# The state-space block's norm worked in pieces inside the first feed-forward, with its input weights fused there and its residual bias added chunk by chunk

## The reference

```
x = x + attention(layernorm(x))
x = x + experts_0(layernorm(x))      # 8 experts, top 2, and a shared expert of two halves
x = x + state_space(layernorm(x))
x = x + experts_1(layernorm(x))
layernorm(x) = (x - mean) / sqrt(var + 1e-5)
state_space(x):  h = x @ fc1_w.T + fc1_b;  xz = h @ in_proj_w.T;  xc, z = split(xz)
                 u = silu(conv over 4 tokens of xc + conv_b)
                 dt, B, C = u @ x_proj_w.T, dt = softplus(dt @ dt_proj_w.T + dt_proj_b)
                 scan over tokens;  y = (y + u * D) * silu(z)
                 return y @ out_proj_w.T @ fc2_w.T + fc2_b
```

## Time and profile before

| | |
|---|---|
| median of 3 runs | 1396.83 us |
| profiled execution, its own time | 1397.44 us |
| its span, first to last instruction | 1395.6 us |
| mean granted clock of PE | 0.937 |
| busy in the span: PE, DVE, ACT, POOL | 88%, 78%, 61%, 41% |
| feed-forward, from about 500 to 749 us of the span | PE 99% busy from 700 to 740 us |
| norm block, 749 to 765 us | PE 8.9, DVE 10.4, ACT 6.1, POOL 8.0 us busy of 16 |

### The profile page before, as it was taken

One profiled execution on the slowest core, in us unless ns is written; L12 is line 12 of the kernel. 1 busy time (PEld: TensorE's weight loads), 2 busy tenths in 40 slices (PEclk: granted clock), 3 DMA queues, 4 the chain that ended last, 5 costly groups with the idle time before them and its releaser, 6 DMA issues. The chain is left out here.

```text
span 1395.6 us, 23364 instructions
## 1 busy us (share of the span) xinstructions
PE 1230.7 (88%) x8438; PEld 643.8 (46%) x8438; DVE 1090.8 (78%) x1318; ACT 851.2 (61%) x1506; POOL 574.8 (41%) x428
## 2 busy tenths in 40 slices
PE   4936999999899989989996866999999999976998
PEld 2411333334333434444543334555555556564665
DVE  5768999989799555867455766999999999864554
ACT  2523899989799742222222678989999899512221
POOL 2320010000100236656665114888888888820000
PEclk9965999999999999999997897999999999985999
DMA  4331111311211165323361001223232223101231
GB/s 111 113 115 31 55 60 48 104 56 55 75 54 50 41 93 143 114 91 113 103 116 23 0 5 49 93 94 100 91 103 94 91 94 103 61 29 24 60 62 38
DMA packets 70525, 103.16 MB, mean 74 GB/s; under 512 B 12598, under 2 KB 42246, under 8 KB 70422
## 3 DMA queue, kind: packets, MB, share of 16 engines
q1 hardware_dynamic: 69126, 100.47, 25.1%
q10 hardware_dynamic: 1296, 1.33, 0.4%
HBM read 88.00 MB, written 13.37 MB: 73 GB/s over the span
## 5 line engine op out<-in xcount | busy, mean ns | idle before, releaser
L638 DVE TENSOR_REDUCE att_found<-PS 128x2 f32<-128x1024 f32 (+2 forms) x288 | 333.2, 1218 | 20.9 <-PE PS L747 19.0
L714 ACT ACTIVATE att_prob<-PS 128x512 f32<-128x512 f32 x576 | 313.6, 596 | 46.1 <-PE PS L769 34.4
L1930 POOL TENSOR_TENSOR ms_ch<-xnT,ms_c_rows 128x1024 f32<-128x1024 f32 x103 | 243.7, 2367 | 45.4 <-PE PS L1840 33.3
L1840 PE MATMUL PS<-ms_ch,ident_sb 128*128 128x512 f32 x512 | 241.2, 593 | 1.0 <-POOL ms_ch L1930 1.0
L1891 DVE TENSOR_TENSOR_SCAN xnT<-xnT,PS 128x1024 f32<-128x1024 f32 x103 | 231.0, 2267 | 7.2 <-PE PS L1831 7.1
L1869 ACT ACTIVATE ms_scaled<-m_dtu_turns,m_bt 128x256 f32<-128x256 f32 x448 | 191.6, 495 | 29.3 <-PE PS L1831 29.3
L788 PE MATMUL PS<-att_prob,att_v 128*32 128x256 f32 (+1 forms) x2560 | 185.0, 376 | 2.8 <-ACT fr_out L703 2.6
L1831 PEld LDWEIGHTS PS<-ident_sb,ms_scaled 128*128 128x128 f32 x1024 | 119.3, 142 | 81.4 <-DVE xnT L1891 37.9
L747 PE MATMUL PS<-kr,qr 55*128 55x128 bf16 (+4 forms) x1152 | 121.7, 293 | 31.0 <-PEq L260 15.8
L1831 PE MATMUL PS<-ident_sb,ms_scaled 128*128 128x128 f32 x1024 | 135.4, 276 | 11.1 <-ACT ms_scaled L1869 5.6
L1262 ACT ACTIVATE f_h<-PS,e_w_b 128x512 f32<-128x512 f32 x64 | 44.0, 687 | 140.1 <-PE PS L1413 136.9
(11 more groups left out here) (225 smaller groups left out, 1724.9 us busy)
## 6 DMA issues: line engine op xcount, KB each, us to landing
ms_c_rows<-bc_rows_dram SPq DMA_DIRECT2D x64, 512.0 KB, 3.7
f_gate_row<-gate_rows_dram SPq DMA_DIRECT2D x64, 256.0 KB, 3.5
f_mask_row<-mask_rows_dram SPq DMA_DIRECT2D x64, 128.0 KB, 3.1
...
```

The lines of the kernel that those rows point to most:

```text
L638: dve.tensor_reduce(found[:, :, pair, first:first + (n - 1) * step + 1:step], PS[:, bank:bank + 2, :].rearrange("p r (w n) -> p r w n", w= ...
L714: act.activation(prob[:, step % PROB_RING * GH + h, :], PS[:, SCORE_BANK + unit % SCORE_RING, :], ACT.Exp, scale=float(D) ** -0.5).then_in ...
L1840: last = pe.matmul(PS[:, Y_BANK + 2 * half + q, :], g.ident[:, :], ch[:, half, q * CH:(q + 1) * CH], start=n == 0, stop=n == NS - 1)
L1930: pool.tensor_tensor(ch[:, half, :], decay_then_h(s, half), c_rows[:, s % C_RING, :], ALU.mult).then_inc(ch_ready, 1)
```

## The change

Four things are done.

1. The norm of the state-space block is taken out of its own block. For sequences 0, 1 and 2 it is done by `Front` in the feed-forward, as batches 4, 5 and 6, in chunks 5, 6 and 7: moments at experts 1 and 2, root on POOL behind the sum of expert 3, two tiles on DVE at each of experts 5, 6, 7 and the next chunk's 0, transposes at that chunk's experts 0 and 2, stores at 2 and 4. Batch 7 (sequence 3) follows behind the last chunk, and so do the last two tiles, the transposes and the stores of batch 6.
2. The weights fc1, in_proj, fc1_b, conv_w and conv_b are loaded by SP at the start of the feed-forward into a new SBUF row (`shared_row`), and the fused weights are computed at chunk 4: PE at expert 0, ACT's copies at expert 2.
3. The other weights of the state-space block are loaded by SP at the start of `mamba_in`, and its engines wait for them behind the convolution.
4. POOL adds fc2_b to X in eight pieces, one behind each `m_dt`.

```diff
     def turn_bank(self, b, k):
-        return (k, 2 + k, k, 1 - k)[b]
+        return (k, 2 + k, k, 1 - k)[b] if b < B else k
...
+    def normalize_half(self, dve, b, k, part):
+        dve.wait_ge(self.rstd_ready, b + 1)
+        dve.wait_ge(self.transposed, CPB * (b - 1) + k + 1)
+        self.normalize_tiles(dve, b, k, range(part * TPC // 2, (part + 1) * TPC // 2))
...
+        if b >= B:
+            pe.wait_ge(self.x_stored, CPB * (b - 1) + k + 1)
...
+        NORM_AT = 5
+
+        def norm_slot(b):
+
+            return NE * (NORM_AT + b - B)
...
         def _(sp):
+            for dst, src in early.pairs:
+                sp.dma_start(dst, src).then_inc(early.loaded, 16)
             for c in range(NCH):
...
+                    if c >= NORM_AT and e == 3:
+                        f.root(pool, B + c - NORM_AT)
+            f.root(pool, 2 * B - 1)
...
+                    if (c, e) == (4, 2):
+                        act.wait_ge(fused, 1)
+                        act.activation(early.in_proj.rearrange("p a b -> p (a b)"), PS[:, FUSED, :], ACT.Copy).then_inc(fused_stored, 1)
+                        act.activation(early.b_in_x, PS[:, FUSED_B, 0:2 * DI], ACT.Copy).then_inc(fused_stored, 1)
+                    for b in range(B, 2 * B - 2):
+                        for part in range(CPB):
+                            if 0 <= e < NE and NE * c + e == norm_slot(b) + 10 + 2 * part:
+                                f.store_x(act, b, part)
             chunks(act, chunk)
+            for b in range(2 * B - 2, 2 * B):
+                for part in range(CPB):
+                    f.store_x(act, b, part)
...
+                for b in range(B, 2 * B - 1):
+                    slot = NE * c + e - norm_slot(b)
+                    if slot == 1:
+                        f.moments_half(dve, b, stats_ready)
+                    if slot == 2:
+                        f.moments_rest(dve, b)
+                    if 5 <= slot < 9:
+                        f.normalize_half(dve, b, (slot - 5) // 2, (slot - 5) % 2)
...
             staggered(dve, chunk)
+            f.normalize_half(dve, 2 * B - 2, 1, 1)
             finish(NCH - 1)
             stats(NCH - 1)
-            dve.wait_ge(stats_ready, NCH)
+            f.moments(dve, 2 * B - 1, stats_ready)
+            for part in range(CPB):
+                f.normalize(dve, 2 * B - 1, part)
...
+                    if (c, e) == (4, 0):
+                        pe.wait_ge(early.loaded, early.all)
...
+                        pe.matmul(PS[:, FUSED, :], early.fc1, early.in_proj.rearrange("p a b -> p (a b)"), start=True, stop=True)
+                        for j in range(2 * DI):
+                            last = pe.matmul(PS[:, FUSED_B, j:j + 1], early.in_proj[:, j, :], early.fc1_b, start=True, stop=True)
+                        last.then_inc(fused, 1)
...
+                    for b in range(B, 2 * B - 2):
+                        for part in range(CPB):
+                            if NE * c + e == norm_slot(b) + 8 + 2 * part:
+                                f.turn_x(pe, b, part)
...
             staggered(pe, chunk)
+            for part in range(CPB):
+                f.turn_x(pe, 2 * B - 2, part)
             finish(NCH - 1, 1)
+            for part in range(CPB):
+                f.turn_x(pe, 2 * B - 1, part)
...
-            pool.tensor_tensor(g.X[:, :, :], g.X[:, :, :], fc2_b[:, :].rearrange("p (a e) -> p a e", a=1).to_broadcast([P, NT, E]),
-                               ALU.add).then_inc(pool_seen, 1)
-
             for c in range(NCH):
                 pool.wait_ge(top_ready, c + 1)
                 pool.wait_ge(soft_steps, 3 * (c + 1))
                 pool.tensor_tensor(m.dt[:, :, tokens(c)], top[:, c % 2, :, :], soft[:, c % 2, :, :], ALU.add).then_inc(dt_ready, 1)
+                x = g.X[:, TPC * c:TPC * (c + 1), :]
+                pool.tensor_tensor(x, x, fc2_b[:, :].rearrange("p (a e) -> p a e", a=1).to_broadcast([P, TPC, E]), ALU.add).then_inc(pool_seen, 1)
...
                 m = mamba_loads(nc, scope, inner, g)
-                norm_transpose(nc, g, 1, [m, m.last])
-                mamba_in(nc, g, m)
+                mamba_in(nc, g, m, early)
```

More of the change, by code:

```diff
@@ L222, in make_globals @@
     g.half = sb("half", [P, NT])
+    g.shared_row = sb("shared_row", [P, T])
     g.PS = ctx.enter_context(nc.psum_tensor("PS", [P, 8, BANK], F32))
@@ L1019, in normalize, with normalize_tiles @@
             dve.wait_ge(self.transposed, CPB * (b - 1) + k + 1)
-        for j in range(TPC):
+        self.normalize_tiles(dve, b, k, range(TPC))
+    def normalize_tiles(self, dve, b, k, tiles):
+        for j in tiles:
             n = TPC * k + j
-            last = dve.tensor_scalar(self.xn[:, k, j, :], self.g.X[:, TB * b + n, :], self.mean[:, n:n + 1], self.rstd[:, n:n + 1],
+            last = dve.tensor_scalar(self.xn[:, k, j, :], self.g.X[:, TB * (b % B) + n, :], self.mean[:, n:n + 1], self.rstd[:, n:n + 1],
                                      ALU.subtract, ALU.mult)
-        last.then_inc(self.normed, 1)
+        if tiles[-1] == TPC - 1:
+            last.then_inc(self.normed, 1)
+    def normalize_half(self, dve, b, k, part):
+        dve.wait_ge(self.rstd_ready, b + 1)
+        dve.wait_ge(self.transposed, CPB * (b - 1) + k + 1)
+        self.normalize_tiles(dve, b, k, range(part * TPC // 2, (part + 1) * TPC // 2))
     def route(self, dve, b, done):
@@ L1468, with mamba_early @@
 LOW_AT = (4 * NS, 6 * NS)
+def mamba_early(nc, ctx, g):
+    m = Loads(nc, ctx, "me_w")
+    row = g.shared_row
+    m.fc1, m.in_proj, m.fc1_b = row[:, 0:P], row[:, P:5 * P].rearrange("p (j c) -> p j c", c=P), row[:, 5 * P:5 * P + 1]
+    at = 5 * P + 1
+    m.conv_w, m.conv_b = row[:, at:at + DI * KC].rearrange("p (d t) -> p d t", t=KC), row[:, at + DI * KC:at + DI * (KC + 1)]
+    at += DI * (KC + 1)
+    m.b_in_x = row[:, at:at + 2 * DI]
+    for name in ("fc1", "in_proj", "fc1_b", "conv_w", "conv_b"):
+        m.to(dict(fc1=m.fc1, in_proj=m.in_proj, fc1_b=m.fc1_b, conv_w=m.conv_w, conv_b=m.conv_b)[name], g.w[name])
+    return m
 def mamba_loads(nc, ctx, early, g):
@@ L1545, in _ @@
         def _(sp):
+            for group in (m, m.last):
+                for dst, src in group.pairs:
+                    sp.dma_start(dst, src).then_inc(group.loaded, 16)
             for c in range(NCH):
@@ L1567, in _ @@
             act.preload_act_table(ACT.Silu)
-            act.wait_ge(m.loaded, m.all)
+            act.wait_ge(early.loaded, early.all)
             act.wait_ge(pad_set, 1)
             act.sem_inc(xc_ready, 1)
-            act.wait_ge(fused, 1)
-            act.activation(w_in_x[:, :, :].rearrange("p a b -> p (a b)"), PS[:, 6, :], ACT.Copy).then_inc(fused_stored, 1)
-            act.activation(b_in_x[:, :], PS[:, 7, 0:2 * DI], ACT.Copy).then_inc(fused_stored, 1)
-            act.wait_ge(fused_stored, 2)
             def take_x(b, k, c):
@@ L1599, in _ @@
             act.preload_act_table_set("natural_log_exp_and_others")
+            act.wait_ge(m.loaded, m.all)
             act.activation(m.a[:, :, :], a_log[:, :, :], ACT.Exp).then_inc(a_steps, 1)
@@ L1643, in _ @@
             dve.sem_inc(conv_steps, 2 * CONV)
-            dve.wait_ge(m.loaded, m.all)
+            dve.wait_ge(early.loaded, early.all)
             with dve.Fori(0, B) as b:
@@ L1707, in _ @@
             pe.sem_inc(z_ready, 2)
-            pe.wait_ge(m.loaded, m.all)
-            pe.matmul(PS[:, 6, :], fc1[:, :], in_proj[:, :, :].rearrange("p a b -> p (a b)"), start=True, stop=True)
-            for j in range(2 * DI):
-                last = pe.matmul(PS[:, 7, j:j + 1], in_proj[:, j, :], fc1_b[:, :], start=True, stop=True)
-            last.then_inc(fused, 1)
-            pe.wait_ge(fused_stored, 2)
             with pe.Fori(0, B) as b:
@@ L1727, in _ @@
             pe.wait_ge(z_ready, 2 + NCH)
+            pe.wait_ge(m.loaded, m.all)
             def low_rank(c):
@@ L2263, in program @@
                 attention(nc, g, weights, f)
-            first_ffn(nc, g, first, f)
+            first_ffn(nc, g, first, f, early)
         with ExitStack() as scope:
-            with ExitStack() as early:
-                m = mamba_loads(nc, scope, early, g)
-                norm_transpose(nc, g, 1, [m, m.last])
-                mamba_in(nc, g, m)
+            with ExitStack() as inner:
+                m = mamba_loads(nc, scope, inner, g)
+                mamba_in(nc, g, m, early)
             mamba_scan(nc, g, m)
@@ L2273, in program @@
             weights = second_loads(nc, scope, g)
[L2274 removed]
+            norm_transpose(nc, g, 1, [weights.route, weights], route=weights.route)
             route_second(nc, g, weights)
```

49 lines of the change are left out of this document (29 added, 20 removed).

## The result

The changed kernel takes 1403.49 us in the median of 4 runs (1402.27 to 1406.01), the kernel before 1396.57 beside it (4 runs); the ratio is 1.0062 with a 95% interval of 1.0039 to 1.0084. In a second comparison on another chip it is 1.0063 (1.0042 to 1.0084). It is slower, by 5 to 12 us and by 8.7 at the ratio; the forecast was 1403.0 against 1396.8, slower with 0.60.

The account below looks back on a forecast made before the run. PE bounds the feed-forward, DVE the state-space block's convolution, and the norm between is a chain. Seven terms, -11.8+2.1+1.8+0.9+10.7+1.3+1.1 = +6.1, on 1396.8 gave 1402.9, say 1403; range 1391 to 1411.

Parts of the forecast that it names:

- 1 norm chain: Between feed-forward and state-space block: the norm block goes, 21.3 us shrinks to 9.5 for batch 7; -11.8.
- 2 five loads: Feed-forward start: five weight loads on SP ahead of the first gate row delay it; +2.1, bounds 0 and 4.
- 3 fused weights: Chunk 4: the fused weights take PE half of 3.54 us at full clock; +1.8.
- 4 transposes: Chunks 6 and 7: four transpose groups on PE at 0.43 each, two hidden in a stall; +0.9.
- 5 moments and tiles: Batches 4 to 6: DVE's norm pieces wait for POOL and stall PE, 3.6 per batch; +10.7, bounds 0 and 17.1.
- 6 tail: Feed-forward's end: later POOL sum, batch 6's last two tiles and four transposes delay PE's last output group; +1.3.
- 7 bias: State-space block: of POOL's eight bias pieces only the last delays DVE's mi_dtu; +1.1, bounds 0 and 4.
- w - 1.67: Feed-forward experts: PE's stall in us when DVE does extra work w behind f_prod.
- w - 0.63: After expert 6: PE's stall, as the next second matmul comes 2.05 later instead of 2.57.
- Rival B: Feed-forward: each batch costs what batch 3 did, or POOL falls behind with f_xm; sum +12.5, 1409; chance 0.12.
- Rival A: Experts 2, 5 and 6: the norm pieces fit DVE's gaps without stalls; sum -4.6, 1392; chance 0.24.
- Rival C: Feed-forward: only the moments or only the tiles stall (4 to 6 us); sum about 0, 1397; chance 0.16.

Follow-up runs that it names:

- tiles in fours: The changed kernel with batches 4 to 6 normalized four tiles at expert 5 and four at expert 6, not in pairs; ratio 1.0116 to the kernel before.
- tiles in pieces of one: The changed kernel with tiles of batches 4 to 6 in pieces of 1, 1, 1 and 5, transposes and stores later; ratio 1.0028 to the kernel before.

## Why the prediction was right

The terms, with what the stretches and the experiments show of each:

| term | forecast | measured |
|---|---|---|
| 1 norm chain | -11.8 | -12.9 |
| 2 five loads | +2.1 | +2.5 |
| 3 fused weights | +1.8 | +1.8 |
| 4 transposes | +0.9 | +1.8 |
| 5 moments and tiles | +10.7 | +9.3 (3.5 and 5.9) |
| 6 tail | +1.3 | +0.7 |
| 7 bias | +1.1 | +3.5 |
| sum | +6.1 | +6.7 |

The moments' price is what their move to expert 1 saved. With them gone, 29.96 less 27.13 is left per chunk, 2.83: two groups of transposes (0.44 each by the distances of the second matmuls, so 1.8 for four) and the tiles, 1.95 per batch. The tail is the remainder of 11.8, the sum of four differences of the table. The ratio gives 8.7 with an interval of 5 to 12 and so holds the 6.7; what lies between is not placed, but the clock above and the last stretch of the table can move a time by more. That the sum came within 0.6 us is luck in part: the terms are off by up to 2.4, and terms 2, 4 and 7, forecast too low, make up for terms 1, 5 and 6.

The mechanism was right in the main. **Term 1**: the first matmul doesn't wait for ACT's table load, as I had it: it starts at 771.10, and the load ends at 771.69. **Term 2**: right, though the first two traces alone would have refuted it. **Term 4**: mis-sized; I let half of the groups vanish in stalls, and the moments' stall is indeed shorter in chunk 6, which has transposes at expert 2, than in chunk 5, which has none (0.51 and 0.85). But when the moments' stall is taken away the groups' full price is there, so it belongs to the one or the other, not to neither. **Term 5**: the formula w - 1.67 and the variant w - 0.63 are right to 0.1 where they can be checked, in the change and in tiles in fours (w of 4.80 and 2.97 give 3.13 and 2.34, measured 3.03 and 2.23). What was off is w: the second pair's was 1.49 and not 1.7, the moments' 2.67 and not 2.95, and the first pair's 3.31 and not 2.9, because DVE waited 0.81 for the root where I had 0.45. The doubt in the forecast that its working was high by a third came of the idle column: batch 3's 2.22 leaves out the wait for f_xm and the 0.16, and from start to start (590.98 to 596.68, 5.70 instead of 2.57) that stall is 3.13, where the working gave 3.2. The moments' blocked steps were the third and fourth of the four, the first being free. **Term 7** was the step that failed: 1.1 us, for the last piece alone. The upper bound of 4 named the mechanism (half a microsecond on each of the others), and that is what came: +3.5 in this stretch, of which the last piece is 1.05. What should have decided it is that mi_dtu and m_dt work on SBUF on both engines in all eight chunks, and each waits for the other. The range too was added up short: B with the bounds of parts 2 and 7 is 12.5 + 1.9 + 2.9 = 17.3 and not +14.

Of what I said the profile would show: the waits for f_prod grew by 6.0 in the idle column, not 10; from start to start the nine second matmuls come 9.2 later in all, the waits for f_xm included; fr_xn took 0.88 a tile in 700 to 740 us (0.9 said); adds 4 to 6 are 31.04 and 30.94 apart (30 to 31). The first f_xm came 6.94 behind the first shared matmul instead of 6.54, and 1.9 later than in the kernel with the loads later. **Rival A** fell as a whole, but tiles in pieces of one show where it begins: 1.15 of work behind f_prod costs 0.08. **Rival B** fell with the stalls of 0.7 to 0.9, though a part of it came: POOL was late with f_xm behind each root, by 0.37. Tiles in fours bring part 5 to 9.3 + 8.2 = 17.5, 1.7 of it the clock, where B had 17.1, so B is about what the old pieces would have cost. **Rival C** fell: both moments and tiles stall.

The Trainium skill's rule that the first starter holds the ports for the whole instruction (SBUF — State Buffer, "Who interferes with whom") can now be weighed. For the tiles no effect of it shows: POOL's sum that starts while a tile runs keeps its 1.26 to 1.27. For the longer pair it agrees, to 0.2: mi_dtu runs from 856.31 to 858.09, the m_dt that starts at 857.17 takes 3.13, and alone m_dt takes 2.00, so 1.13 stand against an overlap of 0.92.
